# First attention of a four-layer kernel: most of the output projection as fp16 products of two parts

## The reference, cut to what matters

```python
q, k, v = (einsum('bsd,hed->bhse', layernorm(x), w) for w in (wq, wk, wv))
scores = where(causal, einsum('bhse,bhte->bhst', q, k) / sqrt(64), -1e9)
heads = einsum('bhst,bhte->bhse', softmax(scores), v)
x = x + heads.transpose(0, 2, 1, 3).reshape(b, s, 1024) @ wo.T     # the projection
```

## Time and profile before

| | |
|---|---|
| median of 3 runs | 959.6 us (958.02 to 961.42) |
| the profiled execution: own time / span | 960.92 us / 959.1 us |
| busy over the span: PE, DVE, ACT, POOL | 84%, 71%, 50%, 43% |
| one block in the middle of the first attention | 29.6 us |
| in it PE, DVE, ACT, POOL busy | 29.10, 20.82, 21.41, 13.89 us |
| TensorE's granted clock, mean / in that block | 0.918 / 1.00 |

### The profile page before, as it was taken

One profiled execution on the slowest core, in us unless ns is written; L12 is line 12 of the kernel. 1 busy time (PEld: TensorE's weight loads), 2 busy tenths in 40 slices (PEclk: granted clock), 3 DMA queues, 4 the chain that ended last, 5 costly groups with the idle time before them and its releaser, 6 DMA issues.

```text
span 959.1 us, 25499 instructions
## 1 busy us (share of the span) xinstructions
PE 804.7 (84%) x10228; PEld 617.0 (64%) x10228; DVE 683.1 (71%) x1560; ACT 479.5 (50%) x817; POOL 409.3 (43%) x302
## 2 busy tenths in 40 slices
PE   1899999999999999999967875588888888749665
PEld 0688888888888888888856544444555555435435
DVE  4777666776666776677774775459999999866763
ACT  1668766677776777767841522023433343205220
POOL 1445444454444544445450100138778877651000
PEclk9999999999999999999985976689999999957776
DMA  6000000000000000000000000000111111110002
GB/s 267 2 3 1 0 0 0 0 0 0 0 0 0 0 0 0 0 0 0 2 2 1 1 1 1 1 1 12 23 22 17 21 17 22 23 23 0 1 1 88
DMA packets 71587, 13.18 MB, mean 14 GB/s; under 512 B 66432, under 2 KB 70528, under 8 KB 70912
## 3 DMA queue, kind: packets, MB, share of 16 engines
q1 hardware_dynamic: 71552, 12.71, 6.1%
HBM read 8.51 MB, written 4.19 MB: 13 GB/s over the span
## 4 chain that ended last, share of the span: by engine, by line
PE 51%; DVE 16%; POOL 13%; issue 10%; ACT 7%; DMA 2%; POOLq 0%; DVEq 0%; SPq 0%; ACTq 0%
POOL b_w L866 9%; PE PS L527 6%; PE PS L484 5%; PE PS L343 5%; PE PS L345 3%; PE PS L344 3%; PE PS L420 3%; PE PS L520 2%; PE PS L506 2%; POOL rstd L367 2%; DVE a_nm L601 2%; DVE stats L358 2%; PE PS L491 2%; ACT a_ph L556 2%; PE PS L510 2%
## 5 line engine op out<-in xcount | busy, mean ns | idle before, releaser
L634 POOL TENSOR_TENSOR a_pl<-a_p,a_ph 128x1024 f16<-128x1024 f32 (+1 forms) x128 | 210.6, 1646 | 256.9 <-ACT a_ph L556 256.9
L553 ACT ACTIVATE a_p<-PS 128x1024 f32<-128x1024 f32 (+1 forms) x128 | 103.7, 810 | 75.3 <-PE PS L491 75.3
L866 POOL TENSOR_TENSOR b_w<-b_v,b_e 128x2048 f32<-128x2048 f32 x32 | 137.7, 4305 | 7.7 <-ACT b_e L781 7.7
L601 DVE TENSOR_REDUCE a_nm<-PS 128x4 bf16<-128x512 f32 (+1 forms) x128 | 121.4, 949 | 0.0
L556 ACT ACTIVATE a_ph<-PS 128x1024 f16<-128x1024 f32 (+1 forms) x128 | 103.0, 805 | 0.0
L546 ACT ACTIVATE a_qk_h<-PS 128x512 f16<-128x512 f32 x128 | 73.3, 603 | 57.1 <-PE PS L345 55.7
L819 DVE TENSOR_TENSOR b_prod<-PS,b_qt 128x512 f32<-128x512 f32 x128 | 83.2, 679 | 15.9 <-PE PS L705 15.1
L366 POOL TENSOR_TENSOR veps<-mv,eps 128x2 f32<-128x2 f32 (+2 forms) x40 | 7.9, 197 | 193.7 <-DVE mv L1140 140.1
L590 DVE TENSOR_TENSOR a_qk_l<-PS,a_qk_h 128x512 f16<-128x512 f32 x128 | 87.0, 681 | 3.4 <-ACT a_qk_h L546 3.4
L703 PE MATMUL PS<-b_kh,w_rolls 128*128 128x256 f16 x256 | 65.1, 282 | 19.3 <-DVE b_prod L819 18.7
L506 PE MATMUL PS<-a_vh,a_ph 128*128 128x65 f16 x768 | 78.5, 196 | 0.3 <-issue 0.3
(11 more groups left out here) (221 smaller groups left out, 2079.6 us busy)
## 6 DMA issues: line engine op xcount, KB each, us to landing
scratch_dram<-b_o SPq DMA_DIRECT2D x32, 64.0 KB, 3.6
b_y<-scratch_dram SPq DMA_DIRECT2D x16, 128.0 KB, 2.1
out_dram<-X SPq DMA_DIRECT2D x2, 1024.0 KB, 3.9
w_rest<-rest_dram SPq DMA_DIRECT2D x1, 1846.0 KB, 15.0
X<-x_dram SPq DMA_DIRECT2D x1, 1792.0 KB, 11.0
w_first<-first_dram SPq DMA_DIRECT2D x1, 1600.0 KB, 6.9
w_rolls<-rolls_dram SPq DMA_DIRECT2D x1, 512.0 KB, 15.4
X<-x_dram SPq DMA_DIRECT2D x1, 256.0 KB, 3.5
```

The source lines that it names most:

```text
L553: act.activation((a_p0, a_p1)[j][:, me, :, :, :].rearrange("p a h q -> p a (h q)"), TT[:, :, 0:512 - 256 * j], ACT.Exp, scale=EA ** -0.5)
L601: dve.tensor_reduce(a_nm[:, nx, j, :].rearrange("p (a h) -> p a h", a=2)[:, :, 0:2], MM[:, :, 0:256 * (j + 1)].rearrange("p a (h k) -> p a ...
L634: pool.tensor_tensor(*(n[:, g % 2, :, :, :].rearrange("p a h q -> p (a h q)") for n in (pl, p, ph)), ALU.subtract).then_inc(a_split, 1)
L866: pool.tensor_tensor(b_w8[:, j, :, :, :], rolled_values(par, j, 0, H), rolled_exps(par, j, 0, H), ALU.mult).then_inc(b_weighed, 1)
```

## The change

Six of the eight chunks of the projection are multiplied as fp16 products of two parts. `a_ot` becomes a buffer of two groups, and GpSimd makes a high and a low part (`a_oh`, `a_ol`) of the copy after groups 2, 3 and 0 (a new step `parts`, in steps g = 2, 3 and 0), at the end of the group's steps. The copy of the last group (chunks 6 and 7) stays f32. The weights `a_wo` are scaled by 32 and split once by GpSimd, in block 0, g = 3 (a new step `weights`). VectorE's addition takes the two factors of 32 out again.

```diff
@@ a_steps
         put(g == 1 and not last, ("xt", 0))
         put(g == 1 and not first, ("project", 0))
+        put(first and g == 3, ("weights", 0))
+        put(g != 1 and not (first and g < 2), ("parts", 0))
         put(last and g == 2, ("ffn_stats", 0))
@@
-A_EPILOGUE = [("normal", 0, 0), ("turn", 0, 0), ("pv", 0, 0), ("pv", 0, 1), ("normal", 1, 0), ("turn", 1, 0),
+A_EPILOGUE = [("normal", 0, 0), ("turn", 0, 0), ("pv", 0, 0), ("pv", 0, 1), ("parts", 0, 0), ("normal", 1, 0), ("turn", 1, 0),
               ("project", 1, 0)]
@@ build
-            a_ot = sb("a_ot", [128, 8, SEQ], stage=in_a)
+            a_ot = sb("a_ot", [128, 2, 2, SEQ], stage=in_a)
+            a_oh, a_ol = sb("a_oh", [128, SPLIT, SEQ], F16, stage=in_a), sb("a_ol", [128, SPLIT, SEQ], F16, stage=in_a)
+            a_wo_h, a_wo_l = sb("a_wo_h", [128, SPLIT, D], F16, stage=in_a), sb("a_wo_l", [128, SPLIT, D], F16, stage=in_a)
@@ a_tensor
                 elif kind == "project":
+                    pe.wait_ge(a_parted, 3 * b)
+                    for t in range(QT):
+                        tok = slice(t * 128, (t + 1) * 128)
+                        for c in range(SPLIT):
+                            mm3(pe, dst[:, tok], a_oh[:, c, tok], a_ol[:, c, tok], a_wo_h[:, c, :], a_wo_l[:, c, :],
+                                t == 0 and c == 0, False)
                     pe.wait_ge(a_turned, GA * b)
                     for t in range(QT):
-                        for c in range(8):
-                            ins = pe.matmul(dst[:, t * 128:(t + 1) * 128], a_ot[:, c, t * 128:(t + 1) * 128],
-                                            w["a_wo"][:, c, :], start=c == 0, stop=c == 7)
+                        tok = slice(t * 128, (t + 1) * 128)
+                        for c in range(SPLIT, 8):
+                            ins = pe.matmul(dst[:, tok], a_ot[:, 1, c - SPLIT, tok], w["a_wo"][:, c, :], start=False,
+                                            stop=t == 1 and c == 7, skip_group_check=True)
@@ a_scalar
                 elif kind == "turn":
-                    c = 2 * ((g - 2) % GA)
-                    act.activation(a_ot[:, c:c + 2, :], src[:, :].rearrange("p (c t) -> p c t", c=2),
+                    if g != 3:
+                        wait(act, a_parted, 3 * b + (-2, -1, 0)[g])
+                    act.activation(a_ot[:, me, :, :], src[:, :].rearrange("p (c t) -> p c t", c=2),
                                    ACT.Copy).then_inc(a_turned, 1)
@@ a_vector
-                    dve.tensor_tensor(xb, R[fill.bank][:, 0:SEQ].rearrange("p (t d) -> p t d", t=QT), xb,
-                                      ALU.add).then_inc(a_added, 1)
+                    dve.scalar_tensor_tensor(xb, R[fill.bank][:, 0:SEQ].rearrange("p (t d) -> p t d", t=QT),
+                                             1.0 / (V_UP * WO_UP), xb, ALU.mult, ALU.add).then_inc(a_added, 1)
@@ a_gpsimd
+                elif kind == "weights":
+                    pool.wait_ge(w_loaded, 16 * 2)
+                    chain.link(pool.tensor_scalar(w["a_wo"], w["a_wo"], WO_UP, None, ALU.mult))
+                    chain.link(pool.tensor_copy(a_wo_h[:, :, :], w["a_wo"][:, 0:SPLIT, :]))
+                    pool.tensor_tensor(a_wo_l[:, :, :], w["a_wo"][:, 0:SPLIT, :], a_wo_h[:, :, :], ALU.subtract)
+                elif kind == "parts":
+                    c = 2 * ((g - 2) % GA)
+                    pool.wait_ge(a_turned, u - 1)
+                    if g == 2:
+                        wait(pool, a_added, b)
+                    ot, oh, ol = a_ot[:, g % 2, :, :], a_oh[:, c:c + 2, :], a_ol[:, c:c + 2, :]
+                    chain.link(pool.tensor_tensor(oh, ot, zeros[:, 0:2].unsqueeze(2).to_broadcast([128, 2, SEQ]), ALU.add))
+                    pool.tensor_tensor(ol, ot, oh, ALU.subtract).then_inc(a_parted, 1)
@@ setup on GpSimd
-            pool.memset(a_vh[:, :, :, :, EA:W], V_UP)
+            pool.memset(a_vh[:, :, :, :, EA:W], 1.0)
```

More of the change, by code:

```diff
@@ L36 @@
 V_UP = 32.0
+WO_UP = 32.0
+SPLIT = 6
 CHUNKS = 2
@@ L402, in build @@
         a_pv, a_normal, a_turned, a_added = sem("a_pv"), sem("a_normal"), sem("a_turned"), sem("a_added")
+        a_parted = sem("a_parted")
         def a_read(step, b):
@@ L513, in do @@
                 elif kind == "turn":
-                    if isinstance(b, int) and b == 0 and g == GA - 1:
-                        pe.wait_ge(w_loaded, 16 * 2)
                     pe.wait_ge(a_normal, u - 1)
@@ L635, in do @@
                                        ALU.subtract).then_inc(a_split, 1)
-            run_plan(pool, A_PLAN, do, chain, 1)
+                elif kind == "weights":
[11 more added lines that the diff above has]
+                    pool.tensor_tensor(ol, ot, oh, ALU.subtract).then_inc(a_parted, 1)
+            run_plan(pool, A_PLAN, do, chain, GA)
         b_filled = sem("b_filled")
```

## The result

The changed kernel has a median of 962.99 us in 11 runs (958.91 to 964.09), the kernel before 958.02 in 11 runs on the same chip. One run of the kernel before took 1174 us and is left out of the ratio, which is 1.0047 [1.0027, 1.0067]. The forecast was 986 and slower. The time is near rival 1's 960 instead, in which the second half of `xn` gets in before GpSimd. The profiled execution took 960.72 us, its span is 958.9 us at a mean granted clock of 0.920, where before had 960.92, 959.1 and 0.918.

A forecast was written before the change was run, and what follows sets the result against it. TensorE was taken to bound the kernel. Matmuls -10.5, epilogue -1.6, collision +33.6, weights +2.5 and last `f_xs` +2.3 gave +26.3 on the profiled 960.9, 987.2, so a median near 986; own range 979 to 995, overall 955 to 996.

The forecast's parts named there:

- rival 1: First attention: second half of `xn` gets in before GpSimd, 14 x 0.54 us, whole 960 us; chance 0.17.
- The step that failed: At `xn`: GpSimd's next instruction runs before the second half, so TensorE waits 2.4 us in 14 blocks, +33.6 us.
- `a_oh` at 1.16 us: GpSimd's first part instruction: 1.16 us, taken from a same-size subtraction, with bounds 0.5 and 2.1 us.
- signs of being wrong: In the profile: `xn` keeps 340 ns, only one half is long, or parts take other than 1.16 us each.
- The matmuls: Projection in blocks 1 to 15: 2.87 us, 0.70 less each, -10.5 us in all.
- The 81 ns of the Trainium skill: Projection's fp16 matmuls: at 81 ns each it would take 3.81 us, the whole 1000; 0.055 us was used instead.
- The collision: At `xn` in blocks 1 to 14: GpSimd holds both halves, TensorE waits 2.4 us each, +33.6 us.
- The weights: Split once on GpSimd in block 0: +2.5 us, bounds 0 and 5.
- The last block's `f_xs`: Its 16 instructions meet two more of GpSimd: +2.3 us, bounds 0 and 2.4.
- The epilogue: Its projection, at the lower clock, takes 5.6 us for 6.48 and its fp16 part starts 0.74 sooner: -1.6 us.

The follow-up runs named there:

- e3: Changed kernel with the high part made by subtracting a full fp16 zero tile, so that instruction takes 1.16 us: 994.88 us, ratio 1.0388.
- e1: Changed kernel with the new matmuls alone, parts set once to constants and no new GpSimd work: 948.73 us, ratio 0.9893.
- e2: Changed kernel with the helper work alone, parts made but unused and the projection f32 again: 972.06 us, ratio 1.0148.
- e4: Changed kernel with the parts of g = 0 made in g = 1 in blocks 1 to 15: 962.79 us, ratio 1.0051.
- e6: Changed kernel with the last block's g = 3 parts held back until VectorE has written `f_xs`: 976.34 us, ratio 1.0211.
- e8: Changed kernel with ScalarE writing `a_oh` in place of GpSimd: 957.78 us, ratio 0.9997.
- e9: Changed kernel with four chunks in parts for six, and no parts in g = 0: 957.7 us, ratio 1.0002.
- the repeat: The changed kernel unedited, run once more: median 961.84 us in 13 runs, ratio 1.0037; its profiled execution took 977.89 us.
- e5: Changed kernel with the split of the weights moved to the end of the prologue: 969.08 us, ratio 1.0128.
- e10: Changed kernel with GpSimd waiting for `xn` before g = 1's first `exph`, weights split in the prologue, last parts after `f_xs`: 954.65 us, ratio 0.9962.
- e11: Changed kernel with four chunks in parts, none made in g = 0, weights split in the prologue, last parts after `f_xs`: 951.27 us, ratio 0.9925.

## Why the prediction was wrong

**The step that failed** is "So a waiting GpSimd gets its turn after one VectorE instruction. I take it that this happens: ... 14 x 2.4". The mechanism it names is real, and its price was right: e3 has 2.42 us in each block. But it needs GpSimd to be waiting when `a_ol` ends, and that rested on a term that I had to take from the nearest row: `a_oh` at 1.16 us. It takes 1.04. The parts then end about 0.1 us before GpSimd's next instruction becomes ready, where the forecast had them end 0.03 us after that, and the second half of `xn` comes first. A repaired step would have read: if the first part instruction is 0.1 us shorter than the row, rival 1. The prediction named only a longer one (over 1.3 us) as the way there. The earlier trace rows could have warned it: in the trace of before, the `f_xs` ahead of the held one starts at 501.698, GpSimd's 501.82 comes 0.13 us behind that, and this `f_xs` keeps its 0.335 us. GpSimd got in only at the one after it. Two of the prediction's own signs of being wrong came true: only one half of `xn` is long, and one part instruction takes other than 1.16 us.

Point by point:

- *The matmuls*: -0.61 us a block in the changed kernel and -0.60 in e1, for -0.70. The fp16 ones were right (0.0556 for 0.055). The 81 ns of the Trainium skill (TensorE: Matmul & The Clock Gate, "Back-to-back issue gap") do not hold here, by that same 0.0556. The f32 part took 0.95 for 0.89. Term: -9 for -10.5.
- *The collision*: +0.47 us a block for rival 1's 0.54, 6.5 us for 7.6 in all. That the `tensor_scalar` waits until GpSimd's instruction ends is shown by e2, e3 and the changed kernel: the held one ends 0.08 to 0.09 us after GpSimd's.
- *The weights*: +3.5 for +2.5, within its bounds (block 1's cheaper projection and its collision lie in this stretch too, so the sum below counts these two twice, which makes 0.1 us); the first instruction took 2.78 us, more than the two ends that I had for it. In the traces of e2, e3, e4, e6, e8, e9 and the repeat a low clock near 65 us adds to it. Same window of e4, the changed kernel, and e5 with early weights (columns as the earlier trace rows, the clock stands third from the end):

```profile
60.00:76.00 16.00, 11.93 (x161) 9.95 (x160) 9.08 (x13) 5.40 (x10) 11.90 (x11) 0.79 0.01 3
```

```profile
60.00:76.00 16.00, 11.99 (x198) 9.91 (x196) 9.55 (x17) 6.77 (x12) 11.99 (x11) 1.00 0.01 3
```

```profile
60.00:76.00 16.00, 15.23 (x271) 12.69 (x269) 11.41 (x21) 10.32 (x18) 9.01 (x7) 1.00 0.01 3
```

  In the changed kernel's trace TensorE is idle as long as in e4's but keeps its clock, so the median's share of this loss is argued, not shown. What it is worth can be read from traces whose program is the same up to there: from the first `xn` to the first addition it is 56.79 us in the changed kernel, 58.02 in the repeat with 3.4 us of it, and 59.06 in e6 with 6.8 us.
- *The last block's `f_xs`*: +1.77 for +2.3, and e6 takes it away.
- *The epilogue*: -2.4 for -1.6. The fp16 part started as forecast at half clock, 0.107 us a matmul, but the four f32 matmuls took 1.00 us for the forecast 1.62, at the full clock's pace.

The sum by measured sizes: -9 - 2.4 + 6.5 + 3.5 + 1.8 = +0.4, and the profiled pair's first attention shows +0.6. The medians differ by 5.0. The difference between the two could be blocks in which GpSimd is first (1.96 us each, or 3.5 with the low clock behind it) and the low clock at the start; both are seen in other executions of this program or its neighbours, but no trace shows them in a run at the median, so their shares stay open. Also open is what moves the gap by 10 ns between executions of the same program. It goes with the program as well: all six runs of e6 took 974 us or more, and 23 of 24 runs of the changed kernel under 966, though the two programs differ only by a wait in the last block.

## What to carry to other kernels

An engine with idle time is not free: read from its timeline where the hole lies, and which instruction of another engine that it can hold up falls into it. Where the outcome hangs on which of two engines comes first by less than a tenth of a microsecond, a forecast should give both orders, and the kernel should set the order with a wait (e10) or leave out the piece that makes the conflict (e11). Work that is done once belongs into a stretch where its engine waits for loads, and a matmul saving that is right to 0.1 us a block is worth nothing until its helper work is costed at the place where it runs.

## What the hardware showed unexpectedly

- An addition of an f32 tile and a broadcast zero on GpSimd, 512 columns to fp16, takes 1.04 us; a subtraction with a full fp16 tile as the second operand 1.16 (e3). A `tensor_scalar` of 1024 f32 columns in place takes 2.78, longer than the subtraction of the same size (2.12), and a cast of 768 columns 0.82.
- GpSimd can go first although its instruction is listed up to 88 ns after VectorE's (e6); VectorE's then takes up to 2.29 us for 0.34.
- A wait of 2.4 us on TensorE is followed by 3.4 us at 1.2 GHz in 6 of 13 blocks of e3, and by none in the others, with the same program around them.
